# Bounds of the weight chunks reach every partition by two small DMAs instead of a transpose and a product on TensorE

## The chip, the cores and the metric

One core of one Trainium2 chip runs the whole program. The metric is the device time of one execution in microseconds (us). In the text PE is TensorE (PEld its weight loads), DVE is VectorE, ACT is ScalarE, POOL is GpSimd and SP is SyncE, whose queue (SPq) issues nearly all transfers; ACTq are transfers that ScalarE's queue issues.

## The reference

Two layers on x of shape (2, 2048, 512), with a condition vector per batch entry. Only the first product, `h @ up_w.T`, has to do with the change.

```python
scale = cond @ norm_w.T + 1.0
h = x * (scale[:, None, :] * rsqrt(mean(x * x) + EPS))
u = h @ up_w.T                                   # up_w: 4096 x 512
val, gate = split(u, 2)
h = val * gelu(gate)
y = act_quant(h) @ weight_quant(down_w).T + x    # layer 1
# layer 2: per batch entry, weights made from the condition (64 groups "dw"), then
# x + relu(x @ Wd_b + bd) @ Wu_b + bu
```

## The kernel before

**Tiling.** The 4096 tokens are four super blocks `s` of 1024 (two tiles of 512). The 2048 hidden columns are 16 chunks `j` of 128. A *quad* n = 16 s + j is one chunk against one super block; there are 64. Each quad forms seven block products (a Strassen scheme), `product(n, p)` with p = 1 to 7, of six 128x512 f16 matmuls each (lines 1025, 1027, 1029): the operands are split in a high and a low f16 half. In a quad PE runs p = 1, 5, then 3 of the quad before, then 6, then 4 of the quad before, then 2 and 7, and behind them the quad's side work.

**Splitting the weights.** Only in the first super block (quads 0 to 15) is each chunk of `up_w` split: ACT writes the high halves (`u_high(j, part)`, line 773), DVE the low ones (`u_low(j, part)`, line 1336), and in quad n it is chunk n + 1 that they work on. The split scales the chunk by a power of two, taken from the largest row sum of absolute values. `row_sums(j)` (ACT, line 744) leaves one sum per partition in column j of `um`. Then `bounds(n)` (PE, lines 1138 and 1141) transposes that column into one row of a PSUM bank, `power(j)` (DVE, lines 1298 to 1300) takes the row's maximum and its power of two into one element, and the next `bounds` spreads it to all partitions by a product with a row of ones. `u_scale` (DVE, lines 1303 and 1311) makes the multiplier `um_mul` from it; `u_high(j, 0)` on ACT waits for that multiplier. A `bounds` stands at the end of each of the quads 0 to 13.

**The side work.** In quads 2, 4, 5, 7, 9, 10, 12, 14 and 15 PE also runs two groups "dw" (`adapter_group`, line 1070): each uses two tiles of 512 KB of `Wdd` that SP loads into `w_ring` (line 514), and ACT copies each result out of PSUM (`stage_group`, line 857). The side work uses two PSUM banks in turn: `take` waits until the use two before has been emptied. A `bounds` behind two groups thus waits for ACT's copy of the first of them.

**Queues.** Every engine runs its instructions in the written order, SP too. In quads 3 to 10 SP issues `load_d` (512 KB of `down_w`), which from the second one on waits until `down_abs` of the one before is done (ACT, line 850, near the end of ACT's quad), then the store of the chunk's early part (`put_e`, line 458), and behind these the four `Wdd` tiles of the next quad with groups.

**The middle of a quad.** ACT's `seed_b(n)` (line 812) and `keep_p5(n)` (line 819) copy products 1 and 5; `gate2(n - 1)` (line 836) makes the gelu of product 3 of the quad before, and `gate1(n)` (line 828), late in ACT's quad, that of product 2. DVE's `seed_c(n)` (line 1474) waits for product 6, `keep_p5(n)` and `gate2(n - 1)`; product 7 on PE waits for `seed_c(n)`. On DVE `multiply2(n - 1)` (line 1513), which waits for `gate2(n - 1)`, stands ahead of `seed_c(n)`.

Of the kernel before, what the change touches and what calls it, by code (L numbers as in the profile page):

```python
# [8 lines left out]
F32 = mybir.dt.float32  # L9
# [7 lines left out]
P = 128  # L17
# [133 lines left out]
def side_work(n):  # L151

    s, j = divmod(n, NP)
    work = [("dw", g) for g in groups_of_quad(n)]
    if n + 2 < NP:
        work.append(("bounds", n))
    if n == 13:
        work.append(("mean", 0))
    if s + 1 < NSB:
        if j in STAT:  # L160
            work.append(("stat", 2 * s + 2 + STAT[j]))
        if j in SPREAD:
            work.append(("rs", 2 * s + 2 + SPREAD[j]))
    if s > 0 and Y_FIRST <= j < Y_FIRST + 4:
        for m in (2 * (j - Y_FIRST), 2 * (j - Y_FIRST) + 1):
            work.append(("y", 2 * (s - 1) + m // KD, m % KD))
    if n in MID_AT:
        work.append(("mid", MID_AT[n]))
    if n in UP_AT:
        i, ks = UP_AT[n]  # L170
        work += [("up", i, k) for k in ks]
    return work


def aux_plan():

    def mid(i):
        return [("mid", i)]

    def up(i, ks=range(KD)):  # L180
        return [("up", i, k) for k in ks]

    uses = [("scale", 0), ("stat", 0), ("turn", 0), ("bounds", -2)]
    uses += [("dw", g) for g in range(4)] + [("bounds", -1)]
    uses += [("dw", g) for g in range(4, EARLY)]
    for n in range(NQ):
        uses += side_work(n)

    uses += mid(3) + mid(4) + up(3) + up(4, (0, 1)) + mid(5) + up(4, (2, 3)) + up(5, (0, 1))
    uses += mid(7) + up(5, (2, 3)) + up(7, (0, 1, 2)) + mid(6) + up(7, (3,)) + up(6)  # L190
    return {key: n for n, key in enumerate(uses)}


def build(nc, x, cond, norm_w, up_w, down_w, Wd, bd, Wu, bu, Wdd, bdd, Wdu, bdu, out):
    aux = aux_plan()
    aux_keys = list(aux)
    with ExitStack() as ctx:
# [178 lines left out]
        s_umul = sem("s_umul")  # L376
        s_us = sem("s_us")
        s_first_hi = sem("s_first_hi")
        s_first_lo = sem("s_first_lo")
# [39 lines left out]
        def bank_free(key):  # L419
# [6 lines left out]
                "turn": (s_top, 1),  # L426
                "bounds": (s_top, i + 4) if i + 3 < NP else (s_umul, 3 * (i + 2) + 3),
                "mean": (s_mean, 1),
# [295 lines left out]
        def _(act):  # L724
# [15 lines left out]
            def row_sums(j):  # L740
                act.wait_ge(s_u[j % 4], 16 * (j // 4 + 1))
                if j:
                    act.wait_ge(s_um, j)
                act.activation(qscale[:, :], u_raw(j).rearrange("p k m -> p (k m)"), ACT.Abs,
                               accum_out=um[:, j:j + 1]).then_inc(s_um, 1)

            def u_high(j, part):

# [146 lines left out]
            row_sums(3)  # L895
            stage_group(3)
            t_high(0, T1)
            t_high(0, T2)
# [8 lines left out]
            stage_group(7)  # L907
            u_high(1, 3)
            for n in range(1, NQ):
                s, j = divmod(n, NP)  # L910
                last = j == NP - 1 and s + 1 < NSB
                seed_b(n)
                if n == 1:
                    u_high(2, 0)
                    row_sums(4)
                if last:
# [3 lines left out]
                if j in SQUARES and s + 1 < NSB:  # L920
                    square(2 * s + 2 + SQUARES[j][0], SQUARES[j][1])
                keep_p5(n)
                if last:
                    t_high(s + 1, T1)
# [11 lines left out]
                if s == 0 and 1 < j and j + 3 < NP:  # L936
                    row_sums(j + 3)
                absolute1(n - 1)
                if j == 0 or n == 1:
# [30 lines left out]
        def _(pe):  # L970
# [162 lines left out]
            def bounds(n):  # L1133

                ps = take("bounds", n)
                if n + 3 < NP:
                    pe.wait_ge(s_um, n + 4)
                    mm = pe.transpose(ps[0:1, 0:P], um[:, n + 3:n + 4], ident[:, :])
# [78 lines left out]
            for g in range(4, EARLY):  # L1217
                adapter_group(g)
            for n in range(NQ):
                if n:  # L1220
# [9 lines left out]
                for key in side_work(n):  # L1230
# [4 lines left out]
                    elif key[0] == "rs":  # L1235
                        spread_rs(key[1])
                    elif key[0] == "bounds":
                        bounds(key[1])
                    elif key[0] == "mean":
# [42 lines left out]
        def _(dve):  # L1282
# [31 lines left out]
            def u_scale(j, pow_):  # L1314
                aux_ready(dve, "bounds", j - 2)
                u_multiplier(j, pow_)
                u_unscale(j, pow_)

            def u_low(j, part):
# [357 lines left out]
            u_scale(2, bank("bounds", 0)[:, P:P + 1])  # L1677
            power(3)
            moving_sum(0, T4)
            seed_c(1)  # L1680
            u_low(2, 0)
            for n in range(1, NQ):
# [25 lines left out]
                if s == 0:  # L1708
                    if 1 < j and j + 1 < NP:
                        u_scale(j + 1, bank("bounds", j - 1)[:, P:P + 1])  # L1710
                    if 1 < j and j + 2 < NP:
                        power(j + 2)
                    if 1 < j and j + 1 < NP:
                        u_low(j + 1, 0)
# [10 lines left out]
                if n > 1:  # L1725
                    multiply2(n - 1)
                    seed_c(n)
                    multiply1(n - 1)
                    running_max2(n - 1)
# [121 lines left out]
```

## Time and profile before

| | |
|---|---|
| time, median of 3 runs | 866.08 us (865.42 to 867.65) |
| the profiled execution | 866.98 us |
| its span, first to last instruction | 865.2 us |
| PE busy | 846.8 us (98%) |
| DVE busy | 608.4 us (70%) |
| ACT busy | 389.9 us (45%) |
| DMA, mean rate | 212 GB/s |
| granted TensorE clock | 1.000 |

The profiled execution takes 1.8 us more than its span. A row of the timeline is one instruction, or some of the same kind: its start in us from the span's start, its length, engine, line, operation, what it writes and reads, how many, and in brackets how long the engine stood idle before it and who released it. Matmuls overlap: six 128x512 matmuls start 0.215 us apart though each is shown with 0.38 us, so the cost of a piece of work on PE is read from start to start.

### The profile page before, as it was taken

The numbers are of one execution on the slowest core, as the hardware profiler recorded it, in microseconds if no ns is written. First come the engines' busy times: TensorE is split into PE (matmuls) and PEld (weight loads), VectorE is DVE, ScalarE is ACT, GpSimd is POOL, SyncE is SP. The second block draws the span as 40 slices with busy tenths as digits, with TensorE's granted clock in tenths as the row PEclk, the third lists the DMA queues.
The fourth block names the chain that finished last, engine by engine and source line by source line (L and its number), as shares of the span: only waits on it lengthen the run. The fifth ranks groups of instructions, "written<-read, shape, count | busy, mean of one in ns | idle before, by whom it ended". The sixth has DMA issues, their size and how long they took to land.

```text
span 865.2 us, 11930 instructions
## 1 busy us (share of the span) xinstructions
PE 846.8 (98%) x4026; PEld 373.9 (43%) x4026; DVE 608.4 (70%) x942; ACT 389.9 (45%) x632; POOL 73.9 (9%) x79
## 2 busy tenths in 40 slices
PE   6999999999999999999999999999999999999998
PEld 5334444444444444444444444444444444444443
DVE  5997666888897765547886664658986764445986
ACT  5678776767545542216545543216433332214000
POOL 0453223210200000000200000000200000000100
PEclk9999999999999999999999999999999999999999
DMA  9879988659788876556587674634447443432231
GB/s 347 308 242 306 332 282 306 219 174 325 246 297 303 312 252 219 204 192 206 207 309 240 230 277 144 203 108 137 144 133 223 137 160 119 159 104 85 98 122 73
DMA packets 64283, 183.50 MB, mean 212 GB/s; under 512 B 7008, under 2 KB 8032, under 8 KB 64224
## 3 DMA queue, kind: packets, MB, share of 16 engines
q1 hardware_dynamic: 63936, 182.48, 60.5%
q8 instruction: 33, 0.54, 0.3%
q10 hardware_dynamic: 288, 0.26, 0.1%
q14 instruction: 26, 0.21, 0.1%
HBM read 152.31 MB, written 29.36 MB: 210 GB/s over the span
## 4 chain that ended last, share of the span: by engine, by line
PE 90%; ACT 3%; DVE 3%; DMA 2%; issue 2%; SPq 0%; POOL 0%; ACTq 0%; DVEq 0%; POOLq 0%
PE aux_ps L1114 10%; PE b_ps L1025 9%; PE b_ps L1029 9%; PE b_ps L1027 9%; PE a_ps L1025 6%; PE a_ps L1027 6%; PE a_ps L1029 6%; PE aux_ps L1070 6%; PE aux_ps L1177 3%; PE aux_ps L1168 3%; PE c_ps L1029 3%; PE c_ps L1027 3%; PE c_ps L1025 3%; PE e_ps L1027 3%; PE e_ps L1029 3%; PE e_ps L1025 3%
## 5 line engine op out<-in xcount | busy, mean ns | idle before, releaser
L1513 DVE SCALAR_TENSOR_TENSOR h_ring<-v_sb,unscale,gelu 128x512 f32<-128x512 f32 x63 | 48.4, 768 | 97.7 <-ACT gelu L836 54.8
L812 ACT ACTIVATE b_ps<-a_ps 128x512 f32<-128x512 f32 x63 | 36.7, 582 | 152.7 <-PE a_ps L1029 152.7
L1025 PE MATMUL b_ps<-t_mov,u_l 128*128 128x512 f16 x252 | 95.5, 379 | 1.6 <-DVE c_ps L1474 1.6
L1029 PE MATMUL b_ps<-t_mov,u_l 128*128 128x512 f16 x252 | 95.5, 379 | 0.0
L1027 PE MATMUL b_ps<-t_mov,u_l 128*128 128x512 f16 x252 | 95.5, 379 | 0.0
L1537 DVE TENSOR_TENSOR hmax<-gelu,hmax 128x512 f32<-128x512 f32 x120 | 82.4, 687 | 6.6 <-ACT gelu L842 1.0
L1114 PE MATMUL aux_ps<-h_ring,wq 128*128 128x512 f16 x384 | 84.9, 379 | 0.3
L711 POOL PARTITION_ALL_REDUCE yscale<-hmax x8 | 17.9, 2266 | 603.0 <-DVE hmax L1537 602.3
L842 ACT ACTIVATE gelu<-h_ring 128x512 f32<-128x512 f32 x64 | 40.3, 630 | 53.0 <-DVE h_ring L1523 52.0
L846 ACT ACTIVATE gelu<-h_ring 128x512 f32<-128x512 f32 x64 | 40.3, 630 | 51.1 <-DVE h_ring L1513 51.1
L1523 DVE SCALAR_TENSOR_TENSOR h_ring<-b_ps,unscale,gelu 128x512 f32<-128x512 f32 x64 | 47.9, 749 | 21.7 <-PE b_ps L1029 21.6
L1070 PE MATMUL aux_ps<-w_ring,cond_sb 128*32 128x512 f32 x480 | 60.4, 599 | 1.0 <-DMA w_ring<-in_Wdd 1.0
L828 ACT ACTIVATE gelu<-a_ps,unscale 128x512 f32<-128x512 f32 x64 | 43.6, 682 | 38.4 <-DVE hmax L1537 35.2
L836 ACT ACTIVATE gelu<-c_ps,unscale 128x512 f32<-128x512 f32 x64 | 43.9, 685 | 32.3 <-PE c_ps L1029 32.3
L1114 PEld LDWEIGHTS aux_ps<-h_ring,wq 128*128 128x128 fp8e4 x384 | 37.3, 98 | 45.8 <-ACT stage L857 1.6
L1570 DVE TENSOR_TENSOR h_ring<-h_ring,qscale 128x1024 f16<-128x1024 f32 x48 | 56.5, 1217 | 0.0
L819 ACT ACTIVATE p_sb<-e_ps 128x512 f32<-128x512 f32 x63 | 37.5, 596 | 39.7 <-PE e_ps L1029 27.6
L1482 DVE TENSOR_TENSOR v_sb<-b_ps,p_sb 128x512 f32<-128x512 f32 x63 | 43.3, 688 | 14.1 <-PE b_ps L1029 13.9
L1596 DVE TENSOR_TENSOR aux_ps<-aux_ps,yscale 128x512 f32<-128x512 f32 x24 | 16.8, 699 | 46.9 <-PE aux_ps L1114 36.9
L1025 PE MATMUL a_ps<-t_mov,u_e 128*128 128x512 f16 x126 | 48.0, 381 | 0.0
L1025 PE MATMUL e_ps<-t_mov,u_e 128*128 128x512 f16 x126 | 47.8, 379 | 0.0
L1027 PE MATMUL e_ps<-t_mov,u_e 128*128 128x512 f16 x126 | 47.8, 379 | 0.0
(217 smaller groups left out, 1640.8 us busy)
## 6 DMA issues: line engine op xcount, KB each, us to landing
w_ring<-in_Wdu SPq DMA_DIRECT2D x64, 512.0 KB, 6.2
w_ring<-in_Wdd SPq DMA_DIRECT2D x56, 512.0 KB, 6.9
u_l<-ul_dram SPq DMA_DIRECT2D x48, 512.0 KB, 4.5
u_e<-ue_dram SPq DMA_DIRECT2D x48, 384.0 KB, 3.1
h_ring<-in_up_w SPq DMA_DIRECT2D x16, 512.0 KB, 7.1
x_sb<-in_x SPq DMA_DIRECT2D x8, 1024.0 KB, 8.1
res<-in_down_w SPq DMA_DIRECT2D x16, 512.0 KB, 6.3
ul_dram<-u_l SPq DMA_DIRECT2D x15, 512.0 KB, 7.6
```

The source lines that it names most:

```text
L828: act.activation(gelu1[:, :], a_ps[n % 2][:, :], ACT.Gelu, scale=unscale[:, s // 2, j:j + 1]).then_inc(s_g1, 1)
L836: act.activation(gelu2[:, :], c_ps[:, :], ACT.Gelu, scale=unscale[:, s // 2, j:j + 1]).then_inc(s_g2, 1)
L1025: pe.matmul(ps[:, :], weight(n, p, 0, k), hi, start=fresh and k == 0, stop=False, skip_group_check=True)
L1027: pe.matmul(ps[:, :], weight(n, p, 0, k), lo, start=False, stop=False, skip_group_check=True)
L1029: mm = pe.matmul(ps[:, :], weight(n, p, 1, k), hi, start=False, stop=k == 1, skip_group_check=True)
L1070: mm = pe.matmul(ps[32 * q:32 * q + 32, :], cond_sb[:, :], w_tile(n)[:, 512 * (q % 2):512 * (q % 2) + 512], start=True, stop=True)
L1114: mm = pe.matmul(ps[:, :], wq[:, c, P * k:P * k + P], q_slot(s, c)[:, TB * t:TB * t + TB], start=(c == 0), stop=(c == NP - 1))
L1482: dve.tensor_tensor(v_sb[:, :], b_ps[n % 2][:, :], p5_sb[:, :], ALU.add)\
L1513: dve.scalar_tensor_tensor(out=h_slot(n)[:, TB:TS], in0=val[:, :], scalar=unscale[:, s // 2, j:j + 1], in1=gelu2[:, :], op0=ALU.mult, op1= ...
L1523: dve.scalar_tensor_tensor(out=h_slot(n)[:, 0:TB], in0=b_ps[n % 2][:, :], scalar=unscale[:, s // 2, j:j + 1], in1=gelu1[:, :], op0=ALU.mul ...
L1537: dve.tensor_tensor(total, absolute, total, ALU.max).then_inc(done, 1)
L1570: dve.tensor_tensor(q_slot(s, c), h_slot(NP * s + c), qscale[:, :], ALU.mult)\
```

## The change

From chunk 3 on the row sums take another way. ACT stores the column of 128 sums to DRAM (`put_bound(j)`, behind `row_sums(j)`), and one quad later loads them back, all 128 to each of the 128 partitions (`get_bound(j)`, 64 KB, behind `keep_p5`), into a part of `wq` that is not in use yet. DVE's `bound_scale(j)` takes the maximum on every partition at once, then the power of two, the multiplier and the unscaling factors. `bounds` stays for n = -2, -1 and 0, and on PE those of quads 1 to 13 are gone. There are 13 stores and 13 loads. Besides, ACT runs `keep_p5(1)` ahead of `u_high(2, 0)` and `row_sums(4)`, and DVE `seed_c(2)` ahead of `u_low(3, 0)`.

```diff
 def side_work(n):
-    if n + 2 < NP:
-        work.append(("bounds", n))
...
+            def put_bound(j):
+                act.wait_ge(s_um, j + 1)
+                act.dma_start(bound_dram[j], um[:, j:j + 1]).then_inc(s_bound_put[j % 2], 16)
+
+            def get_bound(j):
+                act.wait_ge(s_bound_put[j % 2], 16 * ((j - 3) // 2 + 1))
+                act.dma_start(bound_row(j), bound_dram[j].partition_broadcast(P))\
+                    .then_inc(s_bound[j % 2], 16)
...
             row_sums(3)
             stage_group(3)
+            put_bound(3)
...
             u_high(1, 3)
+            get_bound(3)
             for n in range(1, NQ):
                 seed_b(n)
-                if n == 1:
-                    u_high(2, 0)
-                    row_sums(4)
...
                 keep_p5(n)
+                if n == 1:
+                    u_high(2, 0)
+                    row_sums(4)
+                    put_bound(4)
+                elif s == 0 and j + 2 < NP:
+                    get_bound(j + 2)
...
                 if s == 0 and 1 < j and j + 3 < NP:
                     row_sums(j + 3)
+                    put_bound(j + 3)
...
+            def bound_scale(j):
+                dve.wait_ge(s_bound[j % 2], 16 * ((j - 3) // 2 + 1))
+                top = um[:, j:j + 1]
+                link(dve.tensor_reduce(top, bound_row(j), AX_X, ALU.max))
+                link(dve.tensor_scalar(top, top, 1e-30, None, ALU.max))
+                link(dve.tensor_scalar(top.bitcast(I32), top.bitcast(I32), EXP_MASK, None,
+                                       ALU.bitwise_and))
+                u_multiplier(j, top)
+                u_unscale(j, top)
...
                 if s == 0:
                     if 1 < j and j + 1 < NP:
-                        u_scale(j + 1, bank("bounds", j - 1)[:, P:P + 1])
-                    if 1 < j and j + 2 < NP:
-                        power(j + 2)
-                    if 1 < j and j + 1 < NP:
+                        bound_scale(j + 1)
+                    if 2 < j and j + 1 < NP:
                         u_low(j + 1, 0)
...
                     multiply2(n - 1)
                     seed_c(n)
+                    if n == 2:
+                        u_low(3, 0)
```

On PE, at the end of quad 1, the program before ran these rows: the last two matmuls of product 7, the transpose and the product of `bounds(1)`, and the first two matmuls of quad 2.

```order
L1027 MATMUL b_ps<-t_mov,u_l 128x512
L1029 MATMUL b_ps<-t_mov,u_l 128x512
L1138 MATMUL aux_ps<-ident,um 1x128
L1141 MATMUL aux_ps<-small,ones 128x1
L1025 MATMUL a_ps<-t_mov,u_e 128x512
L1027 MATMUL a_ps<-t_mov,u_e 128x512
```

In the changed program (whose line numbers are a little higher) the same place has these rows.

```order
L1048 MATMUL b_ps<-t_mov,u_l 128x512
L1050 MATMUL b_ps<-t_mov,u_l 128x512
L1046 MATMUL a_ps<-t_mov,u_e 128x512
L1048 MATMUL a_ps<-t_mov,u_e 128x512
L1050 MATMUL a_ps<-t_mov,u_e 128x512
```

Quad 2 follows product 7 at once. On ACT, quad 2 before: `seed_b(2)`, `keep_p5(2)`, `u_high(3, 0)`, `gate2(1)`, `u_high(3, 1)`, `absolute2(1)`, `row_sums(5)`, `absolute1(1)`.

```order
L812 ACTIVATE b_ps<-a_ps 128x512
L819 ACTIVATE p_sb<-e_ps 128x512
L773 ACTIVATE u_e<-h_ring,um_mul 128x256
L836 ACTIVATE gelu<-c_ps,unscale 128x512
L773 ACTIVATE u_e<-yscale,um_mul 128x512
L846 ACTIVATE gelu<-h_ring 128x512
L744 ACTIVATE qscale,um<-h_ring 128x1024
L842 ACTIVATE gelu<-h_ring 128x512
```

And ACT's quad 2 of the changed program, with the load of chunk 4's bounds and the store of chunk 5's.

```order
L827 ACTIVATE b_ps<-a_ps 128x512
L834 ACTIVATE p_sb<-e_ps 128x512
L759 DMA wq<-bound_dram 128x128
L788 ACTIVATE u_e<-h_ring,um_mul 128x256
L851 ACTIVATE gelu<-c_ps,unscale 128x512
L788 ACTIVATE u_e<-yscale,um_mul 128x512
L861 ACTIVATE gelu<-h_ring 128x512
L749 ACTIVATE qscale,um<-h_ring 128x1024
L755 DMA bound_dram<-um 128x1
L857 ACTIVATE gelu<-h_ring 128x512
```

Two transfers are issued from ACT's queue in every such quad, one behind `keep_p5` and one behind `row_sums`. On DVE, quad 2 before, from the two `u_low` of chunk 2: multiplier and unscaling of chunk 3, then `power(4)`, `u_low(3, 0)`, `multiply2(1)`, `seed_c(2)`.

```order
L1336 SCALAR_TENSOR_TENSOR u_l<-h_ring,um_mul,u_l 128x512 x2
L1303 TENSOR_SCALAR um_mul<-aux_ps 128x1
L1311 TENSOR_SCALAR unscale<-aux_ps,small 128x1 x2
L1298 TENSOR_REDUCE small<-aux_ps 1x1
L1299 TENSOR_SCALAR small<-small 1x1
L1300 TENSOR_SCALAR small<-small 1x1
L1336 SCALAR_TENSOR_TENSOR u_e<-h_ring,um_mul,u_e 128x256
L1513 SCALAR_TENSOR_TENSOR h_ring<-v_sb,unscale,gelu 128x512
L1474 TENSOR_TENSOR c_ps<-b_ps,p_sb 128x512
```

The same piece of DVE's program after the change.

```order
L1368 SCALAR_TENSOR_TENSOR u_l<-h_ring,um_mul,u_l 128x512 x2
L1344 TENSOR_REDUCE um<-wq 128x1
L1345 TENSOR_SCALAR um<-um 128x1
L1346 TENSOR_SCALAR um<-um 128x1
L1324 TENSOR_SCALAR um_mul<-um 128x1
L1332 TENSOR_SCALAR unscale<-um,small 128x1 x2
L1545 SCALAR_TENSOR_TENSOR h_ring<-v_sb,unscale,gelu 128x512
L1506 TENSOR_TENSOR c_ps<-b_ps,p_sb 128x512
L1368 SCALAR_TENSOR_TENSOR u_e<-h_ring,um_mul,u_e 128x256
```

The count of small operations is the same, but the multiplier of chunk 3 now stands behind the three that find the maximum, and `u_low(3, 0)` behind `seed_c(2)`.

## Rows read from the trace of the kernel before

**Rows 1.** The page: busy time of the engines; the chain that ended last, by engine.

```profile
PE 846.8 (98%) x4026; PEld 373.9 (43%) x4026; DVE 608.4 (70%) x942; ACT 389.9 (45%) x632; POOL 73.9 (9%) x79
PE 90%; ACT 3%; DVE 3%; DMA 2%; issue 2%; SPq 0%; POOL 0%; ACTq 0%; DVEq 0%; POOLq 0%
```

**Rows 2.** Waits of PE from 42 to 200 us: in total, times, longest.

```profile
PE aux_ps L1138 <- ACT stage L857: 3.3, 5, 1.1
PE b_ps L1025 <- DVE c_ps L1474: 1.6, 2, 1.1
PE aux_ps L1070 <- DMA w_ring<-in_Wdd: 1.0, 2, 0.8
PE aux_ps L1102 <- ACT stage L857: 0.2, 1, 0.2
PE aux_ps L1084 <- ACT stage L857: 0.2, 1, 0.2
```

**Rows 3.** Timeline of PE: the bounds of quad 1, the first matmul of quad 2.

```profile
50.14 0.27 PE L1138 MATMUL aux_ps<-ident,um 128*1 128x128 f32 x1
50.65 0.39 PE L1025 MATMUL a_ps<-t_mov,u_e 128*128 128x512 f16 x1
```

**Rows 4.** Timeline of PE at the side work of quad 5.

```profile
95.46 1.92 PE L1070 MATMUL aux_ps<-w_ring,cond_sb 128*32 128x512 f32 x16
98.29 0.27 PE L1138 MATMUL aux_ps<-ident,um 128*1 128x128 f32 x1 [0.90 <-ACT stage L857]
```

**Rows 5.** Timeline of PE at the side work of quads 7 and 9.

```profile
118.45 2.47 PE L1070 MATMUL aux_ps<-w_ring,cond_sb 128*32 128x512 f32 x16
121.28 0.27 PE L1138 MATMUL aux_ps<-ident,um 128*1 128x128 f32 x1 [0.35 <-ACT stage L857]
...
144.41 1.05 PE L1070 MATMUL aux_ps<-w_ring,cond_sb 128*32 128x512 f32 x4 [0.78 <-DMA w_ring<-in_Wdd]
```

**Rows 6.** Timeline of ACT: gate1(1) ahead of seed_b(2), and u_high(3, 0).

```profile
53.21 0.69 ACT L828 ACTIVATE gelu<-a_ps,unscale 128x512 f32<-128x512 f32 x1 [1.48 <-DVE hmax L1534]
...
56.32 0.51 ACT L773 ACTIVATE u_e<-h_ring,um_mul 128x256 f16<-128x256 f32 x1 [1.43 <-DVE um_mul L1303]
```

**Rows 7.** Timeline of DVE in quad 2.

```profile
56.14 0.14 DVE L1303 TENSOR_SCALAR um_mul<-aux_ps 128x1 int32<-128x1 int32 x1
...
56.47 0.27 DVE L1298 TENSOR_REDUCE small<-aux_ps 1x1 f32<-1x128 f32 x1
...
57.02 0.75 DVE L1336 SCALAR_TENSOR_TENSOR u_e<-h_ring,um_mul,u_e 128x256 f16<-128x256 f32 x1
...
58.83 0.68 DVE L1474 TENSOR_TENSOR c_ps<-b_ps,p_sb 128x512 f32<-128x512 f32 x1
```

**Rows 8.** Timeline of ACT in quad 8.

```profile
128.94 0.19 ACT L744 ACTIVATION_READ_ACCUMULATOR qscale<-h_ring 128x1 f32 x1
129.26 0.63 ACT L842 ACTIVATE gelu<-h_ring 128x512 f32<-128x512 f32 x1
...
132.53 0.19 ACT L850 ACTIVATION_READ_ACCUMULATOR res<-res 128x1 f32 x1
```

**Rows 9.** The DMA queue of SP: the Wdd tiles of quads 5 and 9.

```profile
85.61 2.74 SPq L514 DMA_DIRECT2D w_ring<-in_Wdd  x4
...
133.82 2.48 SPq L514 DMA_DIRECT2D w_ring<-in_Wdd  x4
```

**Rows 10.** Windows: us, busy by engine, clock, DMA share, GB/s.

```profile
74.00:97.00 23.00, 21.87 (x118) 9.18 (x116) 17.70 (x38) 19.28 (x34) 6.74 (x8) 1.00 0.99 350
```

**Rows 11.** DMA landing: line 514 from 84 to 97 us; ACT's queue until 40 us.

```profile
DMA to landing us min/median/max: 6.7/7.8/8.4
...
q10 hardware_dynamic: 288, 0.26, 1.9%
cond_sb<-in_cond ACTq DMA_DIRECT2D x1, 1.0 KB, 4.2
```

**Rows 12.** The only small transfer that ACT issues: how long its queue takes.

```profile
1.24 0.44 ACTq L876 DMA_DIRECT2D cond_sb<-in_cond  x1
```

More of the change, by code:

```diff
@@ L184, in aux_plan @@
     uses += [("dw", g) for g in range(4)] + [("bounds", -1)]
-    uses += [("dw", g) for g in range(4, EARLY)]
+    uses += [("dw", g) for g in range(4, EARLY)] + [("bounds", 0)]
     for n in range(NQ):
@@ L205, in build @@
         ul_dram = nc.dram_tensor("ul_dram", [NP, P, 2 * 1024], F16, kind="Internal").ap()
+        bound_dram = nc.dram_tensor("bound_dram", [NP, P], F32, kind="Internal").ap()
         u_e = sb("u_e", [P, 2, 2, 768], F16)
@@ L310, in s_split, with bound_row @@
                 "p (a m) -> p a m", a=2)
+        def bound_row(j):
+            return wq[:, j, :].bitcast(F32)
         v_first = v_sb[:, :].bitcast(F16).rearrange("p (a m) -> p a m", a=4)
@@ L377, in build @@
         s_us = sem("s_us")
+        s_bound_put = [sem(f"s_bound_put{n}") for n in range(2)]
+        s_bound = [sem(f"s_bound{n}") for n in range(2)]
         s_first_hi = sem("s_first_hi")
@@ L426, in bank_free @@
                 "turn": (s_top, 1),
-                "bounds": (s_top, i + 4) if i + 3 < NP else (s_umul, 3 * (i + 2) + 3),
+                "bounds": (s_top, i + 4) if i < 0 else (s_umul, 3 * (i + 2) + 3),
                 "mean": (s_mean, 1),
@@ L1135, in bounds @@
                 ps = take("bounds", n)
-                if n + 3 < NP:
+                if n < 0:
                     pe.wait_ge(s_um, n + 4)
@@ L1218, in _ @@
                 adapter_group(g)
+            bounds(0)
             for n in range(NQ):
@@ L1236, in _ @@
                         spread_rs(key[1])
-                    elif key[0] == "bounds":
-                        bounds(key[1])
                     elif key[0] == "mean":
@@ L1677, in _ @@
             u_scale(2, bank("bounds", 0)[:, P:P + 1])
-            power(3)
             moving_sum(0, T4)
```

## The prediction

> **What bounds the kernel now.** I read the page first: PE is busy 98% of the span and holds 90% of the chain that ended last [rows 1]. So a microsecond taken off PE's own work, or off a wait of PE, counts, unless something stands close behind PE. The change touches quads 0 to 15 (42 to 212 us), so I read the waits of PE there next [rows 2]: 3.3 us at `bounds` for ACT's copy of a dw group, 1.6 us for `seed_c`, 1.0 us for the Wdd tiles. Third, the windows, because two transfers per chunk are added: from 74 to 97 us the DMA engines are busy 0.99 of the time [rows 10]. PE is the bound, but in the quads with dw groups DMA is close behind.
>
> **What is removed.** Start to start, `bounds` holds PE from 50.14 to 50.65, 0.51 us [rows 3]. It is gone from quads 1 to 13; the one of quad 13 has no transpose. That one and the transpose of quad 0's I take as 0.3 and 0.2 us out of the 0.51. Quads 2 to 12 give 11 x 0.51 = 5.6, quad 13 0.3: 5.9 us. With it go the waits for the bank. The 3.3 us are quads 2, 4, 5, 7 and 10; the longest is 1.1, quad 4's [rows 2], and two more stand in the rows: 0.90 and 0.35 [rows 4, 5]. Behind two dw groups the next user of a bank is now the `stat` or `rs` in its place, which waits for the copy of the first group and not of the second, so their 0.2 + 0.2 us [rows 2] go too. Sum for quads 2 to 13: 5.9 + 3.3 + 0.4 = 9.6 us. That is what PE alone would give.
>
> **The two moved operations, quads 0 to 2.** They aim at the 1.6 us of waits for `seed_c` in quads 1 and 2. In quad 1 `keep_p5(1)` comes over a microsecond sooner and product 7 with it. But product 6 of quad 2 then waits for `seed_b(2)`, which stands on ACT behind `gate1(1)`, and that started at 53.21 after 1.48 us of waiting for DVE's first running maximum [rows 6]. The chain to it (a copy by ACT, its low half by DVE, the maximum) does not start sooner: `put_bound(4)` stands in it. So what quads 0 and 1 win (0.7 us of work, up to 0.6 of wait) is lost there. In quad 2, `u_low(3, 0)` leaves the way to `seed_c(2)`, but the multiplier, at 56.14 before, now comes behind the reduction and its two steps, which took 56.47 to 57.02, 0.55 us [rows 7]. ACT waits for just that multiplier (1.43 us, released at 56.32 [rows 6]), `gate2(1)` is behind it, and `seed_c(2)` at 58.83 [rows 7] needs both. The 0.55 us cancel most of the 0.7 us that `u_low(3, 0)` took from 57.02 on [rows 7]. I price quads 0 to 2, apart from the 1.0 us of `bounds` and bank wait counted above, at 0.2 us lost; bounds: 0.8 gained, 0.6 lost.
>
> **What is added on ACT.** The nearest row for issuing a small transfer is 0.44 us of ACT's queue [rows 12]. `put_bound` waits for its own row sum: the accumulator ends at 129.13, the next activation began at 129.26 [rows 8]; with the issue between them it begins near 129.7: 0.4 us later. `get_bound` follows `keep_p5`, where ACT usually waits 0.3 us for product 3 anyway; I take it as hidden, at most 0.4. ACT has room: it is busy 19.3 of 23 us [rows 10], and in the middle of a quad `seed_c` is some 1.5 us ahead of product 7. But SP's `load_d` waits for `down_abs` at the end of ACT's quad (132.72 in quad 8 [rows 8]), and the Wdd tiles stand behind it: they are issued at 133.82 [rows 9], 2.4 us into quad 9. So ACT's 0.4 us make the tiles late.
>
> **What is added on DMA.** Per chunk 128 packets of 4 bytes out and 128 of 512 bytes in. Below: 65 KB at the 350 GB/s of [rows 10], 0.2 us. Above: until 40 us ACT's queue had 288 packets, 1.9% of 40 us x 16 engines [rows 11], 42 ns each, half of them 2 KB; as many packets cost 0.76 us of all engines. I take 0.3, since 4- and 512-byte packets are the cheaper ones.
>
> **Where the tiles take it back.** Three times PE meets tiles that are just in time.
> - Quad 5: the last tile is issued at about 87.8 [rows 9] and lands 8.4 us later [rows 11], 96.2; PE ended the groups at 97.38 [rows 4] and could have at 96.7: slack 0.7. DMA is full from 74 us on, so the tile can come sooner only by what the stretch starts sooner, about 0.5, less two chunks' transfers, 0.6. PE would have come 0.8 + 0.5 + 1.1 + 0.5 = 2.9 us sooner (quad 2's 1.0 less 0.2; quad 3; quad 4) and gets 0.6: 2.3 lost.
> - Quad 7: two groups take 1.92 us when nothing is missing [rows 4], here 2.47 [rows 5]: no slack. Quad 6's 0.51 is lost, and the tiles are 0.4 + 0.3 later: 1.2 lost.
> - Quad 9: PE waits there already [rows 5]; the same sum, 1.2 lost.
> - Quads 12 and 14: I allow 0.6 and 0.1, from load and use times read in the same way (slack 0.6 and 0.3).
>
> Sum: 9.6 - 0.2 - 2.3 - 1.2 - 1.2 - 0.7 = 4.0 us gained. The profiled execution is 866.98 (span 865.2 and 1.8 around it), so 863.0 for its like; it lies 0.9 above the median, and from the median, 866.08, it is **862.1 us**.
>
> **A rule against it.** The row first: ACT's 1 KB transfer of 128 short packets lands after 4.2 us, while SP's first loads are in flight [rows 11]. The Trainium skill, "DMA: Bandwidth & Descriptors", measures 0.68 us for 4 KB and 0.95 us for 64 KB (GpSimd's path), and its Rules say that "under 64 KB you're paying mostly overhead". By that an estimate is 1.6 us of DMA per chunk in place of my 0.3; four paced stretches would cost 6.5 us more, and the time would be near 868. The rows of ACT's queue speak for less, and no row here shows a 4-byte store to DRAM.
>
> **The rivals.**
> - *PE alone decides* (20%). Tiles come sooner with everything else, since SP's waits follow PE too, and the small packets slip in between. For it: DMA idles for microseconds between the paced stretches, and the waits for tiles are only 1.0 us now. Against it: `down_abs` hangs on ACT, which does not get faster. 866.08 - 9.6 = 856.5.
> - *All is taken back* (20%): 0.76 us of DMA per chunk and both issues exposed on ACT (0.8). Quad 5 loses 3.3, quads 7 and 9 0.5 + 0.8 + 0.76 = 2.1 each, quad 12 1.5, the rest 0.5: 9.5 of 9.6, 866.0.
> - *A blocked ACT queue* (10%, slower). `get_bound(j)` waits for the store of the quad before, issued about 7.4 us into that quad; ACT reaches the wait 3.3 us into the next, 5.0 us later where the quad has no dw groups (9.1 us long). If the store lands like SP's tiles in a full queue, 8.2 us, ACT stands 3.2 us, 1.7 more than `seed_c`'s 1.5; behind quads 3, 6, 8 and 11 that is 6.8 us: 866.08 - 4.0 + 6.8 = 868.9. It decides from a landing of 7.5 us on (4 x 1.0 us eat the gain). The 4.2 us of ACT's queue [rows 11] speak against it. The Trainium skill, the same page, "Queues, rings and completion order", says each DMA engine takes the queue rows in turn, packet by packet, so ACT's store would not stand behind SP's backlog; the row agrees.
> - The change does what it says in any case; that only `seed_c`'s move does nothing is part of the forecast.
>
> **How the numbers follow.** My forecast has 50%, with 860 to 863.5 as its own range. A measurement of this kernel tells about 0.3%, 2.6 us, from no change. Faster by more: the forecast and PE alone, 70%; within: 20%; slower: 10%. The range leaves out half of *PE alone* and all of *blocked*: 857.0 to 866.5.
>
> **What the profile would show right or wrong.** No rows of lines 1138 and 1141 after quad 0, and quads without groups 9.1 us long: the removal is right. PE waiting for `w_ring` in quads 5, 7 and 9 with 4 to 6 us in total in place of 1.0 (matmuls stretched by missing tiles included): the pacing is right; none there, and PE alone decides. Product 6 of quad 2 waiting for `seed_b`, and product 7 starting at 59 to 60 us: the early part is right. ACT's gap at the store of 0.4 us, none at the load. If ACT waits for the bounds' store, or DVE for the load, the last rival holds and the prediction is wrong.

## The result, and the profile after

The change makes the kernel 6.5% slower: 924.36 us median of 6 runs (920.24 to 926.09) with 866.61 (865.42 to 870.93) for the kernel before on the same chip, ratio 1.0653, 95% interval 1.0618 to 1.0688. The forecast was 862.1, with a range up to 866.5. The profiled execution has a span of 918.5 us, 53.3 more than before.

The page of the changed kernel: busy time by engine, then the chain that ended last, by engine and by line.

```profile
PE 863.0 (94%) x3987; PEld 372.4 (41%) x3987; DVE 607.6 (66%) x942; ACT 391.2 (43%) x632; POOL 73.0 (8%) x79
...
PE 75%; DMA 14%; DVE 4%; ACT 3%; issue 3%; SPq 2%; ACTq 0%; DVEq 0%
PE aux_ps L1135 9%; PE b_ps L1046 7%; PE b_ps L1048 7%; PE b_ps L1050 7%; DMA bound_dram<-um 7%; DMA w_ring<-in_Wdd 6%; PE a_ps L1046 5%; PE aux_ps L1091 5%; PE a_ps L1048 5%; PE a_ps L1050 5%; PE aux_ps L1199 3%; PE aux_ps L1190 3%; PE e_ps L1046 2%; PE e_ps L1048 2%; PE e_ps L1050 2%
```

Before, PE held 90% of that chain [rows 1]. Now DMA holds 14%, and half of it is the store of the row sums, 13 transfers of 512 bytes.

The waits after, PE and ACT from 42 to 252 us (in total, times, longest), which answer to [rows 2]; then the landing of the 13 stores (line 755) and of the 13 loads (line 759).

```profile
PE b_ps L1046 <- DVE c_ps L1506: 26.1, 9, 6.5
PE aux_ps L1091 <- DMA w_ring<-in_Wdd: 16.6, 11, 5.7
PE b_ps L1046 <- ACT b_ps L827: 0.7, 1, 0.7
...
ACT u_e L788 <- DMA bound_dram<-um: 38.3, 8, 8.4
...
DMA to landing us min/median/max: 8.3/10.5/15.2
...
DMA to landing us min/median/max: 4.7/6.3/7.5
```

The store lands after 10.5 us at the median; the nearest row before was 4.2 [rows 11]. ACT stands 38.3 us for it, product 7 waits 26.1 us for `seed_c`, and the Wdd tiles are missed for 16.6 us where it was 1.0. PE waits 43.4 us in this part in place of 6.3 [rows 2], 37 more. Its busy time is 863.0 in place of 846.8 [rows 1], another 16, though work was taken off it. The two make the 53.3.

One store followed through, timeline of ACT in the changed kernel:

```profile
93.05 0.33 ACTq L755 DMA_DIRECT2D bound_dram<-um  x1
93.42 0.63 ACT L857 ACTIVATE gelu<-h_ring 128x512 f32<-128x512 f32 x1 [0.40 <-ACT qscale L749]
...
107.37 0.33 ACTq L759 DMA_DIRECT2D wq<-bound_dram  x1
107.82 0.51 ACT L788 ACTIVATE u_e<-h_ring,um_mul 128x256 f16<-128x256 f32 x1 [7.31 <-DMA bound_dram<-um]
```

and the same stretch in windows (us; busy by engine; granted clock; DMA share; GB/s):

```profile
96.00:98.00 2.00, 1.88 (x9) 0.57 (x10) 1.92 (x4) 2.00 (x5) 0.50 (x1) 1.00 1.03 395
98.00:100.00 2.00, 2.00 (x11) 0.94 (x10) 1.03 (x7) 1.58 (x4) 1.92 (x3) 1.00 1.50 90
100.00:102.00 2.00, 2.00 (x11) 0.90 (x10) 0.00 (x0) 0.51 (x1) 0.90 (x2) 1.00 1.04 48
102.00:104.00 2.00, 2.00 (x11) 0.87 (x9) 0.00 (x0) 0.00 (x0) 0.00 (x0) 1.00 1.47 58
104.00:106.00 2.00, 1.05 (x5) 0.29 (x3) 0.00 (x0) 0.00 (x0) 0.00 (x0) 1.00 0.79 65
106.00:108.00 2.00, 0.00 (x0) 0.00 (x0) 0.00 (x0) 0.18 (x1) 0.00 (x0) 1.00 0.84 170
108.00:110.00 2.00, 0.00 (x0) 0.00 (x0) 1.48 (x3) 1.73 (x4) 0.00 (x0) 0.64 1.01 386
110.00:112.00 2.00, 1.49 (x4) 0.59 (x5) 1.61 (x3) 1.60 (x4) 0.00 (x0) 0.50 1.06 388
```

For eight microseconds, 98 to 106, all transfers together move 48 to 90 GB/s where they moved 395, while the DMA engines still count as busy. When the store has landed the rate is back. DVE and ACT empty themselves from 100 us on, PE from 105. The granted clock stays at full (2.4 GHz) until PE has idled, and is 0.50, the level of 1.2 GHz, when it starts again: a 128x512 f16 matmul then shows 0.59 us in place of 0.38. PE's busy time grew by such stretches, and by the dw matmuls: the 128 of quads 1 to 15 keep PE busy for 27.9 us in place of 17.9, since they come in pieces as their tiles land and take 720 ns at the mean in place of 599.

### The profile page after: what moved, and what is told of

The parts are those of the page before. It is cut to its first block, busy times and chain, and to the rows that moved or that the text cites. A ratio compares the mean times of both kernels' runs of the same rounds, so it can differ in the third digit from the quotient of the medians.

```text
span 918.5 us, 11865 instructions
## 1 busy us (share of the span) xinstructions
PE 863.0 (94%) x3987; PEld 372.4 (41%) x3987; DVE 607.6 (66%) x942; ACT 391.2 (43%) x632; POOL 73.0 (8%) x79
## 4 chain that ended last, share of the span: by engine, by line
PE 75%; DMA 14%; DVE 4%; ACT 3%; issue 3%; SPq 2%; ACTq 0%; DVEq 0%
PE aux_ps L1135 9%; PE b_ps L1046 7%; PE b_ps L1048 7%; PE b_ps L1050 7%; DMA bound_dram<-um 7%; DMA w_ring<-in_Wdd 6%; PE a_ps L1046 5%; PE aux_ps L1091 5%; PE a_ps L1048 5%; PE a_ps L1050 5%; PE aux_ps L1199 3%; PE aux_ps L1190 3%; PE e_ps L1046 2%; PE e_ps L1048 2%; PE e_ps L1050 2%
## 5 line engine op out<-in xcount | busy, mean ns | idle before, releaser
L1046 PE MATMUL b_ps<-t_mov,u_l 128*128 128x512 f16 x252 | 97.1, 385 | 26.1 <-DVE c_ps L1506 26.1
L1050 PE MATMUL b_ps<-t_mov,u_l 128*128 128x512 f16 x252 | 97.5, 387 | 0.0
L1048 PE MATMUL b_ps<-t_mov,u_l 128*128 128x512 f16 x252 | 97.3, 386 | 0.0
L1091 PE MATMUL aux_ps<-w_ring,cond_sb 128*32 128x512 f32 x480 | 72.1, 631 | 16.8 <-DMA w_ring<-in_Wdd 16.6
L716 POOL PARTITION_ALL_REDUCE yscale<-hmax x8 | 17.9, 2269 | 605.6 <-DVE hmax L1569 605.0
L1368 DVE SCALAR_TENSOR_TENSOR u_e<-h_ring,um_mul,u_e 128x256 f16<-128x256 f32 (+1 forms) x23 | 14.0, 612 | 59.6 <-ACT u_e L788 59.6
L1514 DVE TENSOR_TENSOR v_sb<-b_ps,p_sb 128x512 f32<-128x512 f32 x63 | 43.4, 688 | 14.0 <-PE b_ps L1050 13.8
L1046 PE MATMUL a_ps<-t_mov,u_e 128*128 128x512 f16 x126 | 49.6, 394 | 0.0
L1048 PE MATMUL a_ps<-t_mov,u_e 128*128 128x512 f16 x126 | 49.5, 393 | 0.0
L1050 PE MATMUL a_ps<-t_mov,u_e 128*128 128x512 f16 x126 | 49.5, 392 | 0.0
```

Source lines behind the costliest of these rows:

```text
L1046: pe.matmul(ps[:, :], weight(n, p, 0, k), hi, start=fresh and k == 0, stop=False, skip_group_check=True)
L1048: pe.matmul(ps[:, :], weight(n, p, 0, k), lo, start=False, stop=False, skip_group_check=True)
L1050: mm = pe.matmul(ps[:, :], weight(n, p, 1, k), hi, start=False, stop=k == 1, skip_group_check=True)
L1091: mm = pe.matmul(ps[32 * q:32 * q + 32, :], cond_sb[:, :], w_tile(n)[:, 512 * (q % 2):512 * (q % 2) + 512], start=True, stop=True)
L1514: dve.tensor_tensor(v_sb[:, :], b_ps[n % 2][:, :], p5_sb[:, :], ALU.add)\
```

## The experiments

Seventeen kernels were run. Where it doesn't say otherwise, one is the kernel before with 13 transfers added behind the same `row_sums`; nobody waits for them before the kernel's end (where they write into `wq`, before quad 16), and all the rest is unchanged. Each ratio is to the kernel before timed beside the same kernels, on the same chip; those times differ by up to 0.9 us, so a cost is read from the ratio or from the "before" that goes with it.

**The store alone.**

```diff
+            def probe(j):
+                act.wait_ge(s_um, j + 1)
+                act.dma_start(probe_dram[j], um[:, j:j + 1]).then_inc(s_probe[j % 2], 16)
```

> The kernel before, with the change's 13 stores of the row sums (128 pieces of 4 bytes, each store to 512 bytes of DRAM) issued on ACT at the same places, but nobody waits for them until the end; the bounds still go over TensorE. Theory S (the 4-byte stores themselves hold the DMA engines for some 8 us each): most of the loss comes back without ACT ever waiting, 890 to 920 us, stores landing after 8 to 15 us, the DMA rate under 100 GB/s for microseconds behind each, and Wdd tiles late. Theory Q (the stores only land late because the DMA engines are full, and ACT's wait for them makes the loss): 866 to 870 us, since nobody waits.

929.05 us (927.11 to 932.94) with 867.42 before, ratio 1.0701 (1.067 to 1.0731): 62 us for 13 stores, more than the whole change costs, and above the range expected of it. Nothing is taken off PE here and ACT waits for none of these stores. Waits of PE from 42 to 252 us, the landing of the stores, and two windows:

```profile
PE aux_ps L1081 <- DMA w_ring<-in_Wdd: 43.4, 16, 7.6
PE b_ps L1036 <- DVE c_ps L1485: 1.7, 2, 1.1
...
DMA to landing us min/median/max: 7.9/10.1/14.5
...
96.00:98.00 2.00, 1.44 (x6) 0.14 (x4) 1.73 (x3) 1.51 (x4) 0.82 (x1) 1.00 1.07 381
98.00:100.00 2.00, 0.00 (x0) 0.00 (x0) 0.00 (x0) 0.18 (x1) 1.92 (x4) 1.00 1.30 150
```

The wait moved from `seed_c` to the tiles, and the rate falls here too, to 139 to 184 GB/s from 98 to 106 us. SP is held up with it: the issue of the four tiles that starts at 98.09 takes 10.13 us, where the one before it took 1.93. So ACT's blocked queue decides where the loss shows, not whether there is one.

**The same store with every piece 4096 bytes from the next**, so the 128 pieces of 4 bytes fall in 128 places (`probe_dram` as [NP, P, 1024], target `probe_dram[j, :, 0:1]`).

> As the run with stores alone, but each 4-byte piece goes to a DRAM address 4096 bytes from the next, so no two pieces share a line. If the pieces are slow because all 16 DMA engines write into the same 512 bytes (theory S, line shared), the time falls to 866 to 872 us; if a 4-byte piece to DRAM is slow wherever it goes (theory S, size), it stays within 1% of the run with stores alone. Theory Q: 866 to 870.

869.75 us, ratio 1.0025 (1.001 to 1.0041). The landing:

```profile
DMA to landing us min/median/max: 1.4/3.7/6.5
```

As many pieces, as small, from the same column, issued by the same queue at the same times: 2.3 us in place of 62 (869.75 - 867.42).

**Wide pieces (128 of 512 bytes, 64 KB).**

> As the run with stores alone, but each store is 128 pieces of 512 bytes of ones (64 KB) to its own DRAM rows. Theory S: pieces of 512 bytes are no trouble, 866 to 869 us, landing in 2 to 6 us. Theory Q: the same time as with 4-byte stores, and the same late landing of 8 to 15 us, since the queue is as full.

870.03 us, ratio 1.0027 (1.0012 to 1.0042), landing 3.8 us. 128 times the bytes cost what the spread 4-byte pieces do.

**The loads alone** (13 loads of a constant 512-byte row to 128 partitions).

> The kernel before, with 13 loads of one 512-byte DRAM row to all 128 partitions (the change's second transfer, of a constant row) issued on ACT, waited for by nobody before quad 16. Theory S: 866 to 869 us, the load is harmless. If the load's 128 packets of 512 bytes hold the engines too: over 872 us.

868.9 us, ratio 1.0019 (1.0003 to 1.0034).

**4-byte pieces into one partition of SBUF** (target `wq[0:1, j, :]`).

> As the run with stores alone, but the 128 pieces of 4 bytes go to one partition of SBUF in place of DRAM. If it is DRAM as a target that makes a 4-byte piece slow: 866 to 870 us. If every 4-byte write is slow: near the run with stores to DRAM.

871.0 us with 866.56 before, ratio 1.0054 (1.0036 to 1.0072), landing 3.8 us: 1 us above the range expected. Side by side in SBUF they do no great harm; of the two targets only DRAM shows the loss.

**The two moved operations alone.**

> Only the two moved operations (keep_p5(1) ahead of u_high(2, 0) and row_sums(4); seed_c(2) ahead of u_low(3, 0)), the bounds stay on TensorE. My prediction's reading: the wait moves to product 6 of quad 2, at most 1 us gained, 865.5 to 867. If they gain what they aim at: 864.5 or less.

866.87 us with 866.56 before, ratio 1.0 (0.9988 to 1.0011). The moves are worth nothing, as forecast (0.2 us).

**The path kept, the harmful store taken out.** The changed kernel; from chunk 4 on the store is of 128 rows of 512 bytes of ones, and all loads read chunk 3's row, so the bounds of later chunks are chunk 3's. ACT's waits, the loads and DVE's part stay.

```diff
-                act.dma_start(bound_dram[j], um[:, j:j + 1]).then_inc(s_bound_put[j % 2], 16)
+                if j == 3:
+                    act.dma_start(bound_dram[j], um[:, j:j + 1]).then_inc(s_bound_put[j % 2], 16)
+                else:
+                    act.dma_start(wide_dram[j], ones[:, :]).then_inc(s_bound_put[j % 2], 16)
...
-                act.dma_start(bound_row(j), bound_dram[j].partition_broadcast(P))\
+                act.dma_start(bound_row(j), bound_dram[3].partition_broadcast(P))\
```

> The changed kernel, but from chunk 4 on the store is 128 pieces of 512 bytes (ones, to scratch rows) and every load reads chunk 3's row, so all chunks take chunk 3's bound; ACT still waits for each store. Theory S: the loss is nearly gone, 858 to 872 us, stores landing in 2 to 6 us. Theory Q (ACT's wait for a store in a full queue): 900 or more.

870.26 us with 866.56 before, ratio 1.0039 (1.0027 to 1.0052). Waits of PE from 42 to 203 us, and the landing of the 12 wide stores:

```profile
PE aux_ps L1095 <- DMA w_ring<-in_Wdd: 5.4, 9, 1.5
PE b_ps L1050 <- DVE c_ps L1510: 3.3, 5, 1.1
...
DMA to landing us min/median/max: 1.5/3.9/7.1
```

54 of the 58 us are gone, and no wait of ACT for a store is left. But 3.7 us slower than before is not the 4.0 faster of the forecast either. The one crowded store left, chunk 3's, lands after 8.0 us and is not what keeps it slow: this kernel starts quad 1 at 42.02 us and quad 4 at 71.44, the one without transfers (below) at 42.12 and 71.39.

**Another way to all partitions: GpSimd's all-reduce** in place of both transfers (`um_all[:, j:j + 1]` from `um[:, j:j + 1]`, between its weight sums).

> The changed kernel with the maximum over partitions made by GpSimd (one all-reduce of 128x1 per chunk, behind the weight sums) in place of the store and the load; no transfer is added, and the bounds of quads 1 to 13 are gone from TensorE. If the transfers are all that is wrong with the change: 857 to 863 us (my prediction's 4 us gain or more). If GpSimd is late for bound_scale or its library has to be loaded each time: DVE waits for it, and the time is above 866.

958.74 us with 866.56 before, ratio 1.1072 (1.1044 to 1.11). Timeline of POOL:

```profile
74.23 0.71 POOL L697 TENSOR_TENSOR h_ring<-h_ring 128x256 f32<-128x256 f32 x1 [8.56 <-issue]
...
76.39 0.72 POOL L704 TENSOR_TENSOR h_ring<-h_ring 128x256 f32<-128x256 f32 x1
83.11 0.41 POOL L723 PARTITION_ALL_REDUCE um_all<-um  x1 [5.99 <-issue]
95.03 0.71 POOL L697 TENSOR_TENSOR yscale<-h_ring 128x256 f32<-128x256 f32 x1 [11.51 <-issue]
```

The operation takes 0.41 us, but GpSimd idles 6 us ahead of it without a releaser, and 7.5 to 13.7 us, again without one, before nine of the next ordinary sums. The Trainium skill, "GPSIMD Engine Reference", section "2.1 Instruction dispatch", says that a freshly loaded kernel's first call pays about 6 us; the 5.99 agrees. In this kernel it is paid in nearly every quad, 65.1 us in 11 times from 42 to 252 us, and so is the way back. The sums are late by it: in the same stretch ACT waits 87 us for them before it can split a chunk, and PE 50 us for the split chunks, while DVE waits only 6.7 us for the all-reduce itself. So this run says what the change-over costs, and nothing on the transfers.

**What the pieces must share.** The store of 128 pieces of 4 bytes at five more layouts. 64 bytes and 16 bytes from piece to piece:

> The kernel before with the 13 stores of 128 pieces of 4 bytes added, each piece 64 bytes from the next (8 KB for a store), nobody waiting for them. Theory of the shared line: with all pieces in one 512-byte row the kernel took 929 us, with pieces 4096 bytes apart 870. If pieces disturb each other only when they lie within the same few bytes (under 64), this one stands at 868 to 872 us and the stores land in under 5 us at the median. If what counts is a region of some hundred bytes to a few KB, it stands between 880 and 929 with landings of 8 us and more.

> As the run with 64 bytes between pieces, but 16 bytes (2 KB for a store): four pieces in each 64 bytes. If the loss comes from pieces in the same 64 bytes, about a quarter to all of it is here (880 to 929 us, landings between 4 and 10 us); if it needs pieces that lie side by side in the same 4 to 16 bytes or a whole row in 512 bytes, 868 to 872 us.

Then, since these two cost no more than 1.1 us above the store with 4096 bytes between pieces, nearer ones: groups of eight side by side with a group in each 64 bytes; 8 bytes from piece to piece; and the same 512 bytes as at first, filled in another order (`probe_dram[j].rearrange("a b -> b a")` of [8, 16]).

> The kernel before with the 13 stores of 128 pieces of 4 bytes, eight neighbours side by side (32 bytes) and the next eight 64 bytes on, so each 64 bytes of DRAM take 8 pieces and a store 1 KB. If pieces disturb each other by lying side by side, about as bad as the full row (905 to 930 us, landings of 8 us and more). If 16 pieces, more than one engine's share, have to fall in the same 64 bytes, 868 to 872 us. If it goes by the number of pieces in 64 bytes, something between.

> The same stores with 8 bytes from piece to piece: 8 pieces in each 64 bytes, none side by side, 1 KB for a store. Side by side is what counts: 868 to 872 us. The number of pieces in 64 bytes counts: as the run with groups of eight. 16 bytes apart it was 869.8.

> The same stores, and the same 512 bytes of one DRAM row for the 128 pieces as in the run that stood at 929 us, but in another order: neighbouring partitions lie 64 bytes apart, and each 64 bytes are filled by 16 partitions that are 8 apart. If the shared row or the shared 64 bytes count, in whatever order: 915 to 930 us or more. If only neighbours in the transfer's own order that lie side by side disturb each other: 868 to 872 us.

| layout of the 128 pieces | pieces in 64 bytes | time, us | ratio (95%) | landing, us |
|---|---|---|---|---|
| 4096 bytes apart | 1 | 869.75 | 1.0025 (1.001 to 1.0041) | 3.7 |
| 64 bytes apart | 1 | 869.83 | 1.0044 (1.003 to 1.0058) | 3.6 |
| 16 bytes apart | 4 | 869.79 | 1.0047 (1.003 to 1.0063) | 4.0 |
| 8 bytes apart | 8 | 877.76 | 1.0099 (1.0074 to 1.0124) | 6.1 |
| eights side by side | 8 | 875.73 | 1.0096 (1.0064 to 1.0129) | 7.5 |
| 512 bytes, other order | 16 | 904.55 | 1.044 (1.0402 to 1.0477) | 9.3 |
| 512 bytes in order | 16 | 929.05 | 1.0701 (1.067 to 1.0731) | 10.1 |

The time before is 867.42 us for the first and the last row, 866.41 for 64 and 16 bytes apart, 867.01 for the other three. Lying side by side is not it: eights side by side and 8 bytes apart cost the same by their ratios. Crowding is: with four pieces in 64 bytes the cost is 3.4 us, with eight 9 to 11, with sixteen 38 and 62. The order counts too. The size of the shared unit is not settled, since a crowded store is also a short one here (2 KB, 1 KB, 512 bytes), nor whether it goes by the pieces or by the DMA engines in one unit. The Trainium skill, "DMA: Bandwidth & Descriptors", "Specifications", says that below 512 bytes a transfer is done by reading, changing and writing back. Small pieces alone bear no such price here (the first row); that pieces which change the same unit must follow one another would fit the table, and no run shows it directly.

**What the change is worth without transfers.** The changed kernel with the maximum taken from a constant row in SBUF; the real bounds are left out.

```diff
-                dve.wait_ge(s_bound[j % 2], 16 * ((j - 3) // 2 + 1))
+                dve.wait_ge(s_um, j + 1)
                 top = um[:, j:j + 1]
-                link(dve.tensor_reduce(top, bound_row(j), AX_X, ALU.max))
+                link(dve.tensor_reduce(top, ones[:, :], AX_X, ALU.max))
```

> The changed kernel with no transfers at all: the bound of a weight chunk is taken from a constant row that is already in SBUF, with the same five VectorE instructions behind it; the real bounds are left out. This is what the work taken off TensorE is worth with everything else of the change kept. By the prediction's own terms 9.6 - 0.2 = 9.4 us less than before if no wait grows (857 us); with the rest terms of the prediction for waits on tiles (5.2 us) 861.6 less the transfers' share, about 859 to 862. By the rival theory that the waits for tiles and for the seed of c give all of it back, whatever the transfers do: 865 to 867. The run with wide stores stood at 870.3.

862.46 us with 866.41 before, ratio 0.9957 (0.9945 to 0.997): 4.0 us gained, 2.6 to 4.8 by the interval, and just above the 859 to 862 expected. PE's waits from 42 to 200 us:

```profile
PE aux_ps L1085 <- DMA w_ring<-in_Wdd: 2.9, 6, 0.9
PE b_ps L1040 <- DVE c_ps L1500: 2.0, 4, 1.1
PE b_ps L1040 <- ACT b_ps L827: 0.6, 1, 0.6
```

**Versions that keep the computation.** First the crowded store is replaced by two steps: pieces of 4 bytes into a row of SBUF, then that row to DRAM in one piece, the load half a quad later.

> A repaired path: the 128 values of a chunk go with pieces of 4 bytes into one row of SBUF (harmless in its own run), from there in one piece of 512 bytes to DRAM, and then to all partitions as in the change; the load is issued later in the quad, behind the next chunk's store. All of the computation is kept. If only the 4-byte stores into one DRAM row do the harm, 868 to 872 us, as the run with wide stores (870.3), the store into SBUF landing in about 4 us and VectorE not waiting for the bound. If ScalarE's wait in its queue costs by itself, over 875.

872.79 us with 866.41 before, ratio 1.0072 (1.0059 to 1.0086). 52 us better than the change, and still slower than before. It came out just above the range, and against the expectation DVE waits for the load, 5.3 us in four places, the longest 2.3.

Then no transfer at all: DVE turns the column in 32x32 blocks and takes each block's largest, GpSimd copies the four values to a row of each block, and DVE turns these back.

```diff
+                link(dve.transpose(row[:, 0:32], row[:, 96:128]))
+                dve.tensor_reduce(one, row[:, 0:32], AX_X, ALU.max).then_inc(s_turned, 1)
...
+                link(dve.transpose(spread[:, :], bound_row(j)))
+                link(dve.tensor_reduce(top, spread[:, 0:P:32], AX_X, ALU.max))
```

> The changed kernel with all of its computation and no transfer: VectorE turns the column in blocks of 32 and takes each block's largest, GpSimd copies the four values to one partition and from there to a row in each block (7 small copies, each waiting for the last), and VectorE turns these back, so every partition has the four values. VectorE has some 0.7 us more to do for each chunk than in the changed kernel, GpSimd 1 to 2 us in its idle time. If the transfers' harm is all that separated the change from its forecast, 862 to 865 us, as the run without transfers (862.5 with 866.4 before). If VectorE's added work delays the seed of c, 865 to 870.

868.08 us with 867.01 before, ratio 1.0009 (0.9995 to 1.0023). Its PE waits from 42 to 203 us point at product 7:

```profile
PE b_ps L1070 <- DVE c_ps L1537: 6.1, 5, 3.1
PE aux_ps L1115 <- DMA w_ring<-in_Wdd: 1.3, 4, 0.4
```

and its timeline of DVE shows what stands ahead of the longest one, in quad 2: DVE reaches chunk 3's bound before GpSimd has folded it.

```profile
58.14 0.31 DVE L1374 STREAM_TRANSPOSE wq<-wq 128x128 f32<-128x128 f32 x1 [1.35 <-POOL wq L742]
```

The last one folds chunk 3 some 15 us sooner and turns later chunks at the end of a quad.

> As the fold on VectorE and GpSimd, but chunk 3 is turned and folded some 15 us sooner (before GpSimd's weight sums of chunk 3), the clearing of the scratch rows moves behind GpSimd's sums of chunk 1, and each later chunk is turned at the end of a quad and not ahead of the bound that ScalarE waits for. If the late start and the wait in quad 1 were the difference to the run without transfers, 3 to 4 us less than the fold before it: 863.5 to 865, with product 7 of quad 1 waiting about 1.1 us. If the added 0.4 to 0.7 us of VectorE in each quad is what costs, it stays at 866.5 to 868.

865.92 us (863.68 to 871.41) with 867.17 before, ratio 0.9989 (0.9972 to 1.0005). It is not told apart from the kernel before, nor, since the intervals of the two ratios overlap, from the other fold; and it lies between the two times that the expectation gave to its two readings. The early part did come back: quad 3 starts at 62.84 us, where it was 65.63 in the other fold and 62.31 without transfers. But by the start of quad 15 it is 3.6 us behind the kernel without transfers again (201.76 and 198.21), and product 7 still waits 5.9 us in five places, at most 1.7. What takes the rest was not tried by itself. No version with the computation kept beats the kernel before.

## Why the prediction was wrong

**The step that failed** is the price of the store, in "What is added on DMA": "I take 0.3, since 4- and 512-byte packets are the cheaper ones", between bounds of 0.2 and 0.76 us per chunk. The store alone costs 4.7 us per chunk (61.6 / 13). Both bounds came from packets of other transfers and counted packets and bytes. Neither is what the store costs: with the same packets it takes 0.2 us per chunk spread out (2.3 / 13 in the first row of the table), and 4.7 crowded into 512 bytes of DRAM. No row before showed pieces crowded in DRAM, the prediction said that no row shows a 4-byte store to DRAM, and took the cheap end all the same. The two ends were no bounds, since they rested on a mechanism (so much per packet) that the unseen transfer need not share. (The upper one is also the price of 288 packets; for a chunk's 256 it would be 0.68.)

**The rivals.** *A blocked ACT queue* named the side and the place: `get_bound` waits for the store of the quad before, and it decides from a landing of 7.5 us on; it landed after 10.5. But its price, 6.8 us, counted ACT's stand alone with the other transfers at full rate. The run in which nobody waits for the store loses more than the change does, so the stand is the form of the loss, not its cause. Nor does a full queue make ACT's store late: the spread and the wide stores, issued into the same queues, land after 3.7 and 3.8 us at the median, while tiles of SP took 7.8 [rows 11]. The prediction's sign for this rival, ACT waiting for the store, came true and could not tell the two apart. *All is taken back* and *PE alone decides* are ruled out, the latter also without transfers. The rule weighed against the change (1.6 us per chunk, near 868) was right in sign and too small for the crowded store, too large for the spread one.

**The tiles take back more than forecast.** Without transfers the kernel gains 4.0 us, the very figure of the forecast, but that is luck. The forecast held 2.0 us for the transfers and their issues (0.6 in quad 5, 0.4 + 0.3 in each of quads 7 and 9), which this kernel does not have; its sum without them is 6.0, outside the interval of 2.6 to 4.8. What is right is the mechanism, that quads with tiles give back what PE wins. First matmuls of product 1 of quads 5 to 8, before and without transfers:

```profile
86.29 0.39 PE L1025 MATMUL a_ps<-t_mov,u_e 128*128 128x512 f16 x1
98.80 0.39 PE L1025 MATMUL a_ps<-t_mov,u_e 128*128 128x512 f16 x1
109.30 0.38 PE L1025 MATMUL a_ps<-t_mov,u_e 128*128 128x512 f16 x1
121.79 0.39 PE L1025 MATMUL a_ps<-t_mov,u_e 128*128 128x512 f16 x1
```

```profile
82.87 0.39 PE L1040 MATMUL a_ps<-t_mov,u_e 128*128 128x512 f16 x1
96.71 0.39 PE L1040 MATMUL a_ps<-t_mov,u_e 128*128 128x512 f16 x1
106.59 0.38 PE L1040 MATMUL a_ps<-t_mov,u_e 128*128 128x512 f16 x1
119.42 0.39 PE L1040 MATMUL a_ps<-t_mov,u_e 128*128 128x512 f16 x1
```

Quad 6, without dw groups, takes 0.62 us less (10.50, 9.88). Quad 5 takes 13.84 in place of 12.51, 1.33 more, though 0.51 of work and 0.90 of bank wait are gone: 2.7 us go to tiles (forecast 2.3, and 1.7 without its transfer term). Quad 7 takes 0.34 more (12.49, 12.83), so 1.2 go to tiles (forecast 1.2, and 0.5 without its 0.7). Over all of it, the dw matmuls before (from 44.80 to 203.63 us) and without transfers (44.23 to 199.71), busy and mean, then the idle time ahead of them:

```profile
L1070 PE MATMUL aux_ps<-w_ring,cond_sb 128*32 128x512 f32 x128 | 17.9, 599 | 1.0 <-DMA w_ring<-in_Wdd 1.0
```

```profile
L1085 PE MATMUL aux_ps<-w_ring,cond_sb 128*32 128x512 f32 x128 | 21.1, 600 | 3.1 <-DMA w_ring<-in_Wdd 2.9
```

and quad 5's without transfers, in the timeline, where before one row of 16 took 1.92 us [rows 4]:

```profile
92.03 1.85 PE L1085 MATMUL aux_ps<-w_ring,cond_sb 128*32 128x512 f32 x8
94.17 1.05 PE L1085 MATMUL aux_ps<-w_ring,cond_sb 128*32 128x512 f32 x4 [0.29 <-DMA w_ring<-in_Wdd]
95.72 1.05 PE L1085 MATMUL aux_ps<-w_ring,cond_sb 128*32 128x512 f32 x4 [0.50 <-DMA w_ring<-in_Wdd]
```

The groups wait 1.9 us more, and the same 128 matmuls, each as long, are spread over 3.2 us more, since they come in pieces as the tiles land: 5.1 us for the tiles. The forecast had 2.3 + 1.2 + 1.2 + 0.7 = 5.4 with the transfers and 3.4 without them, so the tiles' own pacing is the stronger by 1.7 us.

**Harmless transfers were too cheap too.** With wide stores the changed kernel takes some 7 us more than with none (ratios 1.0039 and 0.9957, spans 868.7 and 861.4), where the sum held 2.0 for transfers and issues together. By the starts of the quads all but 0.2 of it falls in quads 4, 5, 7, 9 and 12, five of those that take tiles (1.9, 0.8, 2.1, 0.8 and 1.3 us), and nothing in quads 6, 8, 10 and 11. So the place was forecast rightly, and the size was not. Added to the kernel before, where the tiles leave PE some slack, wide stores cost 2.6 us and loads 1.5. So even without crowding the change stands at about 870, and all of its gain and nearly as much again is gone. The change with its own bounds stored 64 bytes apart, and loaded back from there, was not run.

**Smaller points.** As forecast, ACT's gap at the store is 0.40 us, in the timeline above; without transfers quads 3 and 8 are 9.08 us long; and product 6 of quad 2 waits for `seed_b`, 0.72 us. Product 7 was to start at 59 to 60 us and starts at 60.33, after a wait of 2.71 us. ACT had stood 3.71 us for chunk 4's store, ahead of the work that `seed_c(2)` needs. Two rows of PE, then one of ACT:

```profile
53.58 0.38 PE L1046 MATMUL b_ps<-t_mov,u_e 128*128 128x512 f16 x1 [0.72 <-ACT b_ps L827]
60.33 0.38 PE L1046 MATMUL b_ps<-t_mov,u_l 128*128 128x512 f16 x1 [2.71 <-DVE c_ps L1506]
...
57.65 0.51 ACT L788 ACTIVATE u_e<-h_ring,um_mul 128x256 f16<-128x256 f32 x1 [3.71 <-DMA bound_dram<-um]
```

With the wide store in its place the same product starts within the forecast:

```profile
59.13 0.38 PE L1050 MATMUL b_ps<-t_mov,u_l 128*128 128x512 f16 x1 [1.12 <-DVE c_ps L1510]
```

## What to carry to other kernels

A column over partitions, stored to a DRAM row in pieces of 4 bytes, is not a small transfer: it can bring all DMA down to a quarter of its rate and less for 8 us. Lay the pieces 64 bytes apart, or send whole rows, and time one such store beside a busy queue before building on it. Where no row shows an operation, bound it by what could be different in kind, not by the cheapest rows per packet. A sum that comes out right with a term that is not there has another term wrong. And a microsecond taken off the busiest engine is worth only what the next one (here the tiles) lets through: 9.6 us of work and waits gave 4.

## What the runs showed of the hardware

- A store of 128 pieces of 4 bytes into the same 512 bytes of DRAM took 8 to 15 us to land. In the stretch shown all transfers of the core fell from 395 GB/s to 48 to 90 meanwhile, with the store alone from 381 to between 139 and 184. With the pieces 4096 to 16 bytes apart it took 3.6 to 4.0 us at the median, and 13 of them cost 2.3 to 3.4 us. Into one partition of SBUF it landed in 3.8.
- Behind a crowded store SP's issue of four transfers took 10.13 us in place of 1.93.
- Added to the kernel before, a small transfer that was not crowded cost 0.1 to 0.3 us of the total whether it had 512 bytes or 64 KB; in the changed kernel a store and a load with their issues cost 0.55 us per chunk.
- GpSimd's change between sums and an all-reduce cost 6 us one way and 7.5 to 13.7 us of idle time the other.
- When PE came back from idling between 105 and 110 us the granted clock was 0.50 (1.2 GHz), with 0.59 us a 128x512 f16 matmul in place of 0.38.
